# Two attention layers: softmax values and softmax sums in one product, with the quotient taken token by token

## The reference, cut to what matters

```
q, k, v  = heads of xn @ w            # 16 heads, 8 features each
scores   = q k^T / sqrt(8)            # layer 0: + a bias by relative position; layer 1: causal mask
attn     = softmax(scores)
layer 0:   s = (attn v) @ w_out + b_out
layer 1:   new_attn = resid_gain[h] * attn + skip_gain[h] * eye - centre_gain[h] * uniform
           s = (new_attn v) @ cproj_w
```

## Time and profile before

| | us |
|---|---|
| three runs | 1042.18, 1039.54, 1040.69 |
| median | 1040.69 |
| span of the profiled execution | 1042.1 |
| TensorE (PE) busy | 867.5 (83%) |
| VectorE (DVE) busy | 728.4 (70%) |
| ScalarE (ACT) busy | 456.1 (44%) |
| GpSimd (POOL) busy | 393.3 (38%) |
| layer 0's divisions | from 137.1 to 487.1 |
| layer 1's divisions | from 777.3 to 1035.1 |

### The profile page before, as it was taken

One profiled execution on the slowest core, in us unless ns is written; L12 is line 12 of the kernel. 1 busy time (PEld: TensorE's weight loads), 2 busy tenths in 40 slices (PEclk: granted clock), 3 DMA queues, 4 the chain that ended last, 5 costly groups with the idle time before them and its releaser, 6 DMA issues.

```text
span 1042.1 us, 22685 instructions
## 1 busy us (share of the span) xinstructions
PE 867.5 (83%) x7795; PEld 551.3 (53%) x7814; DVE 728.4 (70%) x1177; ACT 456.1 (44%) x808; POOL 393.3 (38%) x421
## 2 busy tenths in 40 slices
PE   1884887999999999987999998525689999999986
PEld 0742443555555555544555555314467667676763
DVE  5564686999899999985665555365456767676763
ACT  1251333545444554533433333258354445454532
POOL 7007772111111111100577776673134334344432
PEclk9996788999999999997999999856899999999998
DMA  4797441332223333204122122240544453435320
GB/s 135 232 142 173 111 113 44 82 75 62 62 63 74 76 81 72 61 7 140 37 59 53 54 56 56 69 125 16 118 98 89 98 103 97 103 97 103 97 44 11
DMA packets 105527, 88.21 MB, mean 85 GB/s; under 512 B 12565, under 2 KB 97497, under 8 KB 102409
## 3 DMA queue, kind: packets, MB, share of 16 engines
q1 hardware_dynamic: 96780, 76.54, 32.4%
q0 software_dynamic: 4352, 8.99, 2.8%
q10 hardware_dynamic: 4352, 2.10, 0.9%
HBM read 45.69 MB, written 41.11 MB: 83 GB/s over the span
## 4 chain that ended last, share of the span: by engine, by line
PE 19%; issue 14%; POOL 8%; DMA 5%; ACT 3%; DVE 3%; SPq 1%; POOLq 0%; ACTq 0%; DVEq 0%
PE ps L666 7%; POOL probs L1137 5%; PE ps L687 3%; DMA ks<-parts_d 3%; PE ps L678 2%; PE ps L660 2%; POOL qkr L1124 1%; ACT rows L888 1%; PE ps L668 1%; POOL qk L1129 1%; DMA parts_d<-qk 1%; PE ps L1469 1%; DVE mx L1191 1%; PE ps L1411 1%; DMA probs<-mixed 0%
## 5 line engine op out<-in xcount | busy, mean ns | idle before, releaser
L1191 DVE TENSOR_REDUCE mx<-ps 128x4 f32<-128x1024 f32 (+1 forms) x224 | 269.5, 1217 | 106.2 <-PE ps L1411 68.4
L1338 ACT ACTIVATE probs<-probs 128x1024 f32<-128x1024 f32 x128 | 135.3, 1057 | 165.6 <-DVE probs L1201 163.1
L1201 DVE TENSOR_TENSOR probs<-ps,tabB 128x1024 f32<-128x1024 f32 x128 | 152.4, 1212 | 3.6 <-PE ps L1431 3.6
L1343 ACT ACTIVATE probs<-ps 128x1024 f32<-128x1024 f32 x96 | 96.5, 1024 | 96.3 <-PE ps L1469 38.6
L1460 PE MATMUL ps<-probs,vpad 128*32 128x256 f32 (+1 forms) x2048 | 132.5, 365 | 3.0 <-ACT probs L1338 1.1
L1137 POOL TENSOR_TENSOR probs<-probs 128x512 f32<-128x512 f32 x64 | 78.9, 1264 | 136.7 <-PE ps L1460 136.7
L1403 PE MATMUL ps<-tabA,eyeb 128*128 128x512 bf16 x256 | 101.9, 398 | 31.2 <-DVE probs L1201 18.0
L1405 PE MATMUL ps<-ks,qs 96*128 96x256 bf16 x512 | 101.7, 281 | 0.0
L1431 PE MATMUL ps<-qs,ks 99*128 99x256 bf16 x512 | 76.7, 279 | 11.1 <-DVE mx L1191 6.0
L666 PE MATMUL ps<-qs,probs 128*128 x144 | 81.7, 650 | 1.4
L1460 PE MATMUL ps<-probs,onespad 128*32 128x256 f32 x1024 | 82.3, 394 | 0.0
(11 more groups left out here) (227 smaller groups left out, 1593.1 us busy)
## 6 DMA issues: line engine op xcount, KB each, us to landing
parts_d<-qk SPq DMA_DIRECT2D x64, 192.0 KB, 2.3
qs<-parts_d SPq DMA_DIRECT2D x32, 384.0 KB, 4.9
ks<-parts_d SPq DMA_DIRECT2D x32, 384.0 KB, 6.7
parts_d<-qk SPq DMA_DIRECT2D x64, 128.0 KB, 1.9
slots_in<-probs SPq DMA_DIRECT2D x1, 4680.0 KB
probs<-slots_in SPq DMA_DIRECT2D x72, 65.0 KB, 1.8
parts_d<-qk SPq DMA_DIRECT2D x64, 64.0 KB, 1.6
probs<-mixed SPq DMA_DIRECT2D x16, 256.0 KB, 3.3
```

What stands on the lines that cost most here:

```text
L1191: nc.vector.tensor_reduce(mx[:, s.buf(), t, heads[0]:heads[-1] + 1], ring[:, slot].rearrange("p (h n) -> p h n", n=w), AX.X, ALU.max).then ...
L1201: nc.vector.tensor_tensor(probs[:, j, :].rearrange("p (h n) -> p h n", n=T), ring[:, slot].rearrange("p (h n) -> p h n", n=T), v.tabB[:, h ...
L1338: nc.scalar.activation(probs[:, j, :], probs[:, j, :], ACT.Exp).then_inc(exp_done, 1)
L1343: nc.scalar.activation(probs[:, j, :], ring[:, slot], ACT.Exp).then_inc(exp_done, 1)
```

## The change

A head's block in `vpad` is now 8 values and 8 ones (16 columns of use in 32), so one product gives both the values and the sums of a head, 16 rows of output. Heads with even i go to the left half (r = 0) of the bank `od`, those with odd i to the right half (r = 1). Rows of values and of sums alternate in `od`, so the quotient can't be taken there. In its place:

1. ScalarE copies the whole bank to SBUF (`copy_products`, 128 x 512), at position 1 in layer 0 and 0 in layer 1.
2. TensorE turns it in four 128 x 128 transposes into `misc` (`tokens_apart`, use "T"), at position 6 in layer 0 and 3 in layer 1. Tokens are now on partitions.
3. VectorE takes 32 reciprocals per partition and one product of 128 x 256 with a broadcast (`divide`), one position later, and writes `onT`.
4. TensorE turns the result back in two transposes into `misc` (`heads_apart`, use "N"), at position 9 and 6.
5. ScalarE copies it to `on` (`quotients`), in layer 1 with the gain as scale, at position 9 and 6.

`add_tiles`, `sums` and their semaphores go; layer 1's exponentials wait for `pv_done` instead of `sum_done`. The first values product of a batch waits for `od_copied` instead of `on_done`. The rows of both output weights and the columns of the skip, centre and gain constants are reordered in `setup` to suit.

```
-        v.vpad = sb("vpad", [P, 3, 8, 160])
-        v.onespad = sb("onespad", [P, 4, 32])
+        v.vpad = sb("vpad", [P, 3, 8, 128])
+        v.nothing = sb("nothing", [P, H, 2])
...
-                (v.wo0[:, :], v.w_out[:, :]),
-                (v.wo1[:, :], v.cproj_w[:, :]),
+                (v.wo0[0:P // 2, :], by_region(v.w_out, 0)),
+                (v.wo0[P // 2:P, :], by_region(v.w_out, 1)),
+                (v.wo1[0:P // 2, :], by_region(v.cproj_w, 0)),
+                (v.wo1[P // 2:P, :], by_region(v.cproj_w, 1)),
...
-    GROUPS = 4
+    APART, BACK = (3, 6) if layer else (6, 9)
...
-    MISC = ["QK", "V", "E", "Y", "M"] if layer else ["QK", "V", "Y", "M"]
-    LAG = {"QK": 1, "V": 0, "E": -2, "Y": -2, "M": 0}
-    EVAC = {"QK": qk_evac, "V": v_evac, "Y": y_evac, "M": mt_evac}
+    MISC = ["QK", "T", "V", "N", "E", "Y", "M"] if layer else ["QK", "V", "T", "N", "Y", "M"]
+    LAG = {"QK": 1, "V": 0, "T": -2, "N": -2, "E": -2, "Y": -2, "M": 0}
+    EVAC = {"QK": qk_evac, "V": v_evac, "T": apart_done, "N": on_done, "Y": y_evac, "M": mt_evac}
...
-        def add_tiles(pool, s, g):
-            pool.wait_ge(pv_done, NU * s.n(-2) + 4 + g // 2 + 1)
-            later = probs[:, g, :].rearrange("p (h t) -> p h t", t=T)[:, :, P:T]
-            second = probs[:, 4 + g // 2, :].rearrange("p (h t) -> p h t", t=P)[:, 4 * (g % 2):4 * (g % 2) + 4, :]
-            nc.gpsimd.tensor_tensor(later, later, second, ALU.add).then_inc(added, 1)
...
             def divide(s):
-                if layer == 0:
-                    dve.wait_ge(pv_done, NU * (s.n(-2) + 1))
-                else:
-                    dve.wait_ge(sum_done, GROUPS * (s.n(-2) + 1))
-                nc.vector.reciprocal(rden[:], od[:, T:2 * T]).then_inc(rd_done, 1)
+                dve.wait_ge(apart_full, s.n(-2) + 1)
+                if s.has(-3):
+                    dve.wait_ge(back_full, s.n(-3) + 1)
+                turned = misc.rearrange("p (g e d) -> p g e d", e=2, d=HD)
+                nc.vector.reciprocal(rden[:], turned[:, :, 1, 0]).then_inc(rd_done, 1)
                 dve.wait_ge(rd_done, s.n(-2) + 1)
-                if s.has(-3):
-                    dve.wait_ge(y_full, s.n(-3) + 1)
-                if layer == 0:
-                    nc.vector.tensor_tensor(on[:], od[:, 0:T], rden[:], ALU.mult).then_inc(on_done, 1)
-                else:
-                    nc.vector.scalar_tensor_tensor(on[:], od[:, 0:T], cols[:, 5:6], rden[:], ALU.mult, ALU.mult
-                                                   ).then_inc(on_done, 1)
+                nc.vector.tensor_tensor(onT[:].rearrange("p (g d) -> p g d", d=HD), turned[:, :, 0, :],
+                                        rden[:].unsqueeze(2).broadcast_to([P, 2 * H, HD]), ALU.mult).then_inc(apart_done, 1)
...
                     if s.has(-2):
-                        act.wait_ge(sum_done, GROUPS * s.n(-2) + (j + 1 if j < 4 else 2 * (j - 4) + 2))
+                        act.wait_ge(pv_done, NU * s.n(-2) + j + 1)
...
+            def copy_products(s):
+                act.wait_ge(pv_done, NU * (s.n(-2) + 1))
+                if s.has(-3):
+                    act.wait_ge(apart_full, s.n(-3) + 1)
+                nc.scalar.activation(ods[:].rearrange("p r t -> p (r t)"), od, ACT.Copy).then_inc(od_copied, 1)
+
+            def quotients(s):
+                act.wait_ge(back_full, s.n(-2) + 1)
+                if s.has(-3):
+                    act.wait_ge(y_full, s.n(-3) + 1)
+                if layer:
+                    nc.scalar.activation(on[:], misc[:, 0:T], ACT.Identity, scale=cols[:, 5:6]).then_inc(on_done, 1)
+                else:
+                    nc.scalar.activation(on[:], misc[:, 0:T], ACT.Copy).then_inc(on_done, 1)
...
                     if s.has(d - 1):
-                        pe.wait_ge(on_done, s.n(d - 1) + 1)
+                        pe.wait_ge(od_copied, s.n(d - 1) + 1)
...
-                for what in range(2 if layer == 0 else 1):
-                    for n, h in enumerate(heads):
-                        i, q = h // 4, h % 4
-                        lhs = vpad[:, b, 4 * c + q, 32 * i:32 * i + 32] if what == 0 else onespad[:, i, :]
-                        mm = nc.tensor.matmul(od[32 * q:32 * q + 32, T * what + t0:T * what + T], lhs,
-                                              probs[:, j, w * n:w * n + w], start=(j == 0 and what == 0 and i == 0),
-                                              stop=(j == NU - 1), skip_group_check=True)
+                for n, h in enumerate(heads):
+                    i, q = h // 4, h % 4
+                    r, first_column = i % 2, 32 * i - 16 * (i // 2)
+                    mm = nc.tensor.matmul(od[32 * q:32 * q + 32, T * r + t0:T * r + T],
+                                          vpad[:, b, 4 * c + q, first_column:first_column + 32],
+                                          probs[:, j, w * n:w * n + w], start=(j == 0 and i == 0),
+                                          stop=(j == NU - 1), skip_group_check=True)
...
-            def sums(s, g):
-                pe.wait_ge(added, GROUPS * s.n(-2) + g + 1)
-                for q in range(4):
-                    mm = nc.tensor.matmul(od[32 * q:32 * q + 32, T:2 * T], onespad[:, g, :], probs[:, g, T * q:T * q + T],
-                                          start=False, stop=(g == GROUPS - 1), skip_group_check=True)
-                mm.then_inc(sum_done, 1)
+            def tokens_apart(s):
+                misc_free(pe, s, "T")
+                pe.wait_ge(od_copied, s.n(-2) + 1)
+                for c in range(2):
+                    for r in range(2):
+                        at = 2 * P * c + P * r
+                        mm = nc.tensor.transpose(misc[:, at:at + P], ods[:, r, P * c:P * c + P], eye)
+                mm.then_inc(apart_full, 1)
+
+            def heads_apart(s):
+                misc_free(pe, s, "N")
+                pe.wait_ge(apart_done, s.n(-2) + 1)
+                for c in range(2):
+                    mm = nc.tensor.transpose(misc[:, P * c:P * c + P], onT[:, P * c:P * c + P], eye)
+                mm.then_inc(back_full, 1)
```

More of the change, by code:

```diff
@@ L65 @@
 C_ALL = C_SPARE + FLIGHT
-W_LOADS, R_LOADS = 14, 5
+W_LOADS, R_LOADS = 16, 5
 PAIR_OF_MINUS_ONES = float.fromhex("-0x1.017f00p+0")
@@ L161, in build @@
         v.mT = sb("mT", [PARTS * 2 * H, P], BF16)
-        v.rden = sb("rden", [P, T])
+        v.ods = sb("ods", [P, 2, T])
+        v.rden = sb("rden", [P, 2 * H])
+        v.onT = sb("onT", [P, T])
         v.on = sb("on", [P, T])
@@ L340, in routing, with by_region @@
             step(nc.vector.tensor_tensor(v.wt[:, 1, :], v.wt[:, 0, :], gap, ALU.mult))
+        def by_region(w, r):
+            return bass.AP(w.tensor, w.offset + r * HD * D, [[2 * HD * D, H // 2], [D, HD], [1, D]])
         @block.sync
@@ L403, in _ @@
             nc.gpsimd.memset(v.vpad[:], 0.0).then_inc(zeroed, 1)
-            nc.gpsimd.memset(v.onespad[:], 0.0).then_inc(zeroed, 1)
+            nc.gpsimd.memset(v.nothing[:], 0.0).then_inc(zeroed, 1)
             pool.wait_ge(zeroed, 8)
-            for i in range(4):
-                nc.gpsimd.memset(v.onespad[:, i, 8 * i:8 * i + 8], 1.0).then_inc(zeroed, 1)
-            pool.wait_ge(zeroed, 12)
+            nc.gpsimd.memset(v.vpad[:].rearrange("p b c (i w) -> p (b c i) w", w=32)[:, :, HD:2 * HD], 1.0).then_inc(zeroed, 1)
+            pool.wait_ge(zeroed, 9)
             nc.gpsimd.memset(v.ks[MROW:P].rearrange("p b h t -> p (b h t)").bitcast(F32), PAIR_OF_MINUS_ONES).then_inc(zeroed, 1)
@@ L522, in _ @@
                     mm.then_inc(lg, 1)
-            pe.wait_ge(copied, 4 + 4 + 13)
+            pe.wait_ge(copied, 4 + 4 + 15)
             for k in range(6):
@@ L1004, in attention @@
     pv_done = sem("pv_done")
-    if layer:
-        added = sem("added")
-        sum_done = sem("sum_done")
+    od_copied = sem("od_copied")
+    apart_full, apart_done = sem("apart_full"), sem("apart_done")
+    back_full = sem("back_full")
     qk_full, v_full = sem("qk_full"), sem("v_full")
@@ L1170, in body @@
             def body(s):
-                if layer and s.has(-2):
-                    for g in range(GROUPS):
-                        add_tiles(pool, s, g)
                 if s.has(1) and (layer or s.k >= LOOP):
@@ L1270, in body @@
                 for pos, (kind, j) in enumerate(U.order):
-                    if layer == 0 and pos == 1 and s.has(-2):
+                    if pos == APART + 1 and s.has(-2):
                         divide(s)
@@ L1276, in body @@
                         maximum_parts(s)
-                    if layer and pos == 4 and s.has(-2):
-                        divide(s)
                     if layer and pos == 7 and s.has(-2):
@@ L1359, in body @@
                 for pos, (kind, j) in enumerate(U.order):
+                    if pos == (0 if layer else 1) and s.has(-2):
+                        copy_products(s)
+                    if pos == BACK and s.has(-2):
+                        quotients(s)
```

(15 more changed lines are left out.)

32 lines of the change are left out of this document (18 added, 14 removed).

## The result

| | before | after |
|---|---|---|
| median of the runs beside each other | 1041.43 (4 runs, 1039.54 to 1050.07) | 1059.63 (4 runs, 1058.65 to 1065.09) |
| span of the profiled execution | 1042.1 | 1056.8 |
| TensorE busy | 867.5 | 816.7 (77%) |
| VectorE busy | 728.4 | 686.7 (65%) |
| ScalarE busy | 456.1 | 486.4 |

The changed kernel is slower: ratio 1.0181, 95% interval 1.0132 to 1.0231. The profiled execution took 1058.65 us. The change did remove work from TensorE, VectorE and GpSimd, 51, 42 and 79 us of it. What came in its place is waiting.

What follows compares the result with a forecast made beforehand. It took layer 0 as bound by TensorE and VectorE close together, with VectorE deciding after the change, and layer 1 by TensorE in program order. 1042.1 + 9 + 9 + 4 - 5 = 1059, less 1.4: 1058 us; range 1022 to 1074.

Steps and rivals of the forecast that it cites:

- Waits in layer 0: Layer 0: VectorE idle 4.1 us a body instead of 2.0, body 23.4 us, 0.6 more; +9 us over 15 bodies.
- the four parts given for A1: Layer 0, before A1: last exponential 1.1, last values product 0.43, QK 0.96, A1 1.08; given as 3.7 us.
- The clock in layer 0: Layer 0: granted clock falls after TensorE's 2.5 us pause before T; 0.65 us a body in 14 bodies, +9 us.
- The half: Layer 0: half of the 1.35 us that T and A4 lose at the low clock, taken as 0.65 us a body.
- Layer 1: Layer 1 bodies: TensorE's path +1.04 us, partly taken up by the 0.77 us pause; +0.3 a body, +4 over 14.
- The end: Kernel's end: one chain falls from 8.1 to 4.6 us, -3.5, and the body before it -1.5; together -5 us.
- The edits at nothing: In `setup`: extra loads, memsets and small VectorE operations lie beside other loads, costing nothing, at most 1 us.
- The small reciprocal: VectorE's division: reciprocal of 32 elements taken as 0.27 us, between an eighth of the large one, 0.22, and 0.42.
- the handing over: Layer 1's division: 0.12 us between reciprocal (0.27) and product (0.42), within 0.8 us in all.
- Clock holds: Rival: waits as forecast in both layers, but the clock does not fall; 1049 us, chance 0.26.
- The bank's turn is not waited for: Rival: no pauses at V and E in layer 1, bodies of 16.1 us, removed work counts; 1028 us, chance 0.2.
- Both clocks: Rival: clock falls in both layers, +12 us in layer 1 and +9 more in layer 0; 1079 us, chance 0.12.

Runs made afterwards that it cites:

- a kernel with the same layer 0: The changed kernel with T and N, in layer 1 alone, written into the values products' bank `od` instead of the shared bank; 1037.06 us, ratio 0.9949.
- the wait alone: The kernel before with one wait added: at position 6 of layer 0 TensorE waits until V is copied out; 1067.14 us, ratio 1.0247.
- the last kernel: The changed kernel with T and N in bank `od` in both layers, layer 0's T at position 1, division ahead of A1, N at 4; 1006.41 us, ratio 0.9683.

## Why the prediction was right

The sum was 1059 - 1.4 = 1058; the median is 1059.63. Its terms, each against what was measured:

- **Waits in layer 0, forecast 0.6 us x 15 = 9.** A body at the full clock takes 23.33 against 22.74: 0.59. The waits are 0.62, 1.91 and 1.30 us for 0.6, 2.0 and 1.4 (the four parts given for A1 add up to 3.57 and not 3.7, which would have made the 2.0 a 1.9); T 0.66 for 0.65, TensorE's pause 2.44 for 2.5, released by the copy of V. Only 11 bodies are steady, so 6.5 us come from them.
- **The clock in layer 0, forecast 0.65 us x 14 = 9.** Over the eleven bodies the excess above 23.33 is 6.0 us, 0.55 each; the experiment that fills the pause puts it at 5.5. The half was a choice and not a reading, so its closeness is luck. The forecast let the clock fall in half of the bodies at 1.35 us each. It falls behind one T in three (276.53, 348.15, 419.80 and one before them) and costs 1.2 us in that body and 0.4 in the next, since it stays low into it. Fewer falls, each a little dearer.
- Both together are 12.5 us in the steady bodies. The stage as a whole is 15.1 us longer, for 18 forecast; the other 2.6 lie in the bodies around them, which the sum had counted as steady ones. That remainder is no firm number: the body ahead of the steady ones took 39.99 us here and 43.94 in a kernel with the same layer 0.
- **Layer 1, forecast 0.3 us x 14 = 4.** 17.78 - 17.49 = 0.29 a body, 3.5 in all. V paused 1.40 for 1.45, E 0.47 for 0.5, and the 0.77 us of slack before A0 was taken up.
- **The end, forecast -5.** It is -5.0. The chain from the copy to the scan takes 4.5 us (1045.82 to 1050.33), for 4.6.
- **The edits at nothing.** The copy of `od` takes 0.60 us beside QK, as said. The small reciprocal was mis-sized: 348 ns for 270, so its time does not go with the element count alone. The division in layer 1 (895.47 to 896.27) still took the 0.8 us of the sum, so the handing over had been put too high by as much; in layer 0 VectorE's next instruction starts 0.72 us after the division does (304.27 to 304.99). Between the layers +1.1 us were not forecast.

The terms sum to 17, the stages of the two profiled executions to 14.7, and the medians differ by 18.2. The two profiled executions are no typical pair. The changed kernel's is the fastest of its four. The one of the kernel before has a span of 1042.1; in every other execution on record but one the time is 1.75 to 1.96 us above the span (1058.65 and 1056.8, 1044.13 and 1042.3, 1007.4 and 1005.6), so its time was, by estimate, 1043.9, above its median. The prediction took the span for the time. That slip did nothing to the forecast, which comes to the median before plus 17 either way. But a single execution is a coarse measure here: the prediction held that two runs can be told apart at 3 us, and 20 further runs of the kernel before lie between 1036.72 and 1048.83. That forecast and median lie within 2 us is therefore better than the terms deserve: both terms of layer 0 were too high by 2 to 3 us in the steady bodies.

The rivals. *Clock holds* (1049) fell: the granted clock is 0.50 from 348 to 354, and filling the pause gains 5.5 us. The Trainium skill ("TensorE: Matmul & The Clock Gate", section "Why this matters for your kernels") asks, of pauses, only that longer ones than this be avoided; the trace disagrees, with a fall behind 2.44 us in one body of three. *The bank's turn is not waited for* (1028) fell, but its size was right: the run with the bank of its own in layer 1 reaches bodies of 16.2 us where the rival had 16.1. *Both clocks* (1079) fell: in layer 1 the window shows 1.00 through pauses of 1.40 and 0.47 us.

The prediction did put the loss down to waits and clock, and not to the change's own work. What it didn't ask is whether T has to stand where it waits: it took the position as given. V's copies end 1.94 us behind B0's bias in the rows it used; two positions later the wait measured 0.20 us.

## What to carry to other kernels

When work moves to another place in a hand-written order, cost the queue for its buffer before the work itself: here 51 us less of TensorE's work in all were outweighed by waits of 2.44 and 1.40 us a body for a bank that another engine empties late. List who holds the shared buffer at each position and when it is let go, then put the new use behind that moment or give it a buffer that is idle anyway. And a wait of the fullest engine has two prices, the time and what a lower clock does to the products behind it.

## What the runs showed of the hardware

- **Useless products paid for themselves.** Six of 512 columns in bf16 (1.46 us) in each pause took the eleven steady bodies from 262.65 to 257.2 us, and no T behind the shortened pause ran at the low clock.
- **The same pause doesn't always end the same.** T behind a pause of 2.44 us took 0.66 us at 301.56 and 1.11 at 348.15. The falls come in a cycle of three bodies (23.33, 24.55, 23.74; with the wait alone 23.61, 26.43, 25.10), one in three after the change and two in three with the wait alone. Why it repeats in threes wasn't tested. With T two positions later no steady body was long. The length of the pause alone doesn't decide: after the change the T at 253.28, 324.90 and 396.55 come behind 2.52 us and take 0.65.
- **The clock fell behind a short pause as well.** Behind 1.04 us of waiting for the last exponential it fell once in eleven bodies with the pause before T filled (287.24) and twice in eleven with T in a bank of its own (255.92 and 279.14), at 1.3 to 1.4 us each. In the last kernel, which has the same 1.04 us, no steady body was long. What decides between them wasn't tested.
- **A small reciprocal isn't an eighth of a large one.** 256 elements per partition took 1756 ns and 32 took 348. By estimate, a line through both has 6.3 ns per element and 0.15 us besides; the small one also reads its elements 16 apart, so the two rows differ in more than size.
